# Strided rows for the blocks of two stacks, and the loads of one of them issued by ScalarE

## What is computed

```python
# layer 0
t  = layer_norm(x, g1, be1)
x  = x + softmax(q(t) @ k(t).T / 4 + mask) @ v(t) @ Wo.T + bo      # 16 heads
x  = x + ctx @ Wg.T + bg
x  = x + relu(layer_norm(x, g2, be2) @ W1.T + b1) @ W2.T + b2
# layer 1
t  = layer_norm(x, ln1_s, ln1_b)
x  = x + softmax(causal(q(t) @ k(t).T / 4)) @ v(t) @ wo
y  = layer_norm(x, ln2_s, ln2_b)
y  = x + softmax(q(y) @ k(ctx).T / 4) @ v(ctx) @ wo
z  = layer_norm(y, ln3_s, ln3_b)
out = y + relu(z @ mlp_w1 + mlp_b1) @ mlp_w2 + mlp_b2
```

## Time and profile before

| | us |
|---|---|
| median of 3 runs | 1675.22 |
| lowest, highest | 1666.01, 1680.92 |
| the profiled execution | 1690.34 |
| its span, first to last instruction | 1688.5 |
| PE, DVE, ACT, POOL busy in it | 1476.3, 1188.2, 1033.3, 837.5 |
| mean granted clock of PE | 0.953 |

### The profile page before, as it was taken

How to read it: one execution, slowest core, us unless ns; L and a number is a source line. 1 busy time by engine, 2 the same in 40 slices (tenths; PEclk the granted TensorE clock), 3 DMA queues, 4 the chain that set the end, 5 groups by cost and what they waited for, 6 DMA issues and landing times.

```text
span 1688.5 us, 43288 instructions
## 1 busy us (share of the span) xinstructions
PE 1476.3 (87%) x13568; PEld 1197.9 (71%) x13568; DVE 1188.2 (70%) x3871; ACT 1033.3 (61%) x2089; POOL 837.5 (50%) x1125
## 2 busy tenths in 40 slices
PE   2799999999999999778877778778999999999986
PEld 1578888888888888655655556555777777777756
DVE  2788878887878887666666666756776777677742
ACT  2677666677767675355545555556566656666652
POOL 4345544455545556643434343535555655565533
PEclk8799999999999999898889999998999999999989
DMA  5654644554555544456564755665644564446400
GB/s 135 151 126 111 130 104 100 118 107 100 126 115 119 115 101 131 104 128 121 103 121 95 129 104 120 136 134 113 117 104 98 117 119 94 105 113 113 86 26 13
DMA packets 163511, 185.76 MB, mean 110 GB/s; under 512 B 15952, under 2 KB 140240, under 8 KB 163408
## 3 DMA queue, kind: packets, MB, share of 16 engines
q1 hardware_dynamic: 163408, 184.57, 51.9%
HBM read 125.78 MB, written 58.72 MB: 109 GB/s over the span
## 4 chain that ended last, share of the span: by engine, by line
PE 55%; DMA 11%; ACT 9%; issue 8%; DVE 7%; SPq 5%; POOL 3%; ACTq 0%; DVEq 0%; POOLq 0%
PE d_ps L447 22%; DMA k_stack<-parts 9%; PE d_ps L708 8%; PE o_ps L582 7%; PE s_ps L504 6%; PE t_ps L518 5%; PE t_ps L552 3%; SPq L409 3%; DMA parts<-q_part 3%; SPq L414 2%; PE m_ps L454 2%; ACT prob_t L756 2%; POOL q_part L1128 1%; ACT q_stack L764 1%; POOL k_f L1128 1%
## 5 line engine op out<-in xcount | busy, mean ns | idle before, releaser
L756 ACT ACTIVATE prob_t<-t_ps 128x384 f32<-128x384 f32 (+1 forms) x512 | 275.4, 551 | 402.6 <-PE t_ps L556 204.0
L504 PE MATMUL s_ps<-k_stack,q_stack 96*128 96x256 bf16 (+1 forms) x1536 | 295.4, 275 | 125.8 <-DMA k_stack<-parts 58.6
L747 ACT ACTIVATE prob<-prob,neg_max 128x256 f32<-128x256 f32 x512 | 232.8, 507 | 124.5 <-DVE neg_max L908 121.6
L504 PEld LDWEIGHTS s_ps<-k_stack,q_stack 96*128 96x128 bf16 x1536 | 116.6, 100 | 228.4 <-issue 74.1
L908 DVE CUSTOM_DVE_ANT_0 prob<-s_ps,bias_sb 128x256 f32<-128x256 f32 x512 | 193.5, 417 | 55.3 <-PE s_ps L504 45.8
L552 PE MATMUL t_ps<-q_stack,k_stack 108*128 108x256 bf16 (+1 forms) x1024 | 209.3, 271 | 23.3 <-ACT prob_t L756 14.7
L1128 POOL TENSOR_TENSOR h_lo<-h_f,h_hi 128x512 fp32r<-128x512 f32 x128 | 164.9, 1288 | 123.1 <-DVE h_hi L1023 123.1
L908 DVE CUSTOM_DVE_ANT_0 prob<-s_ps,causal 128x128 f32<-128x128 f32 (+1 forms) x512 | 158.4, 351 | 93.8 <-PE s_ps L504 91.3
L893 DVE TENSOR_REDUCE top<-s_ps 128x2 f32<-128x512 f32 x256 | 172.9, 682 | 55.6 <-PE s_ps L504 51.8
L582 PE MATMUL o_ps<-prob_t,v_sb 128*17 128x256 f32 (+1 forms) x3072 | 204.2, 387 | 0.0
L447 PE MATMUL d_ps<-x2t_hi,w_hi 128*128 128x256 f32 x512 | 156.9, 306 | 14.8 <-ACT k_f L827 9.8
(11 more groups left out here) (127 smaller groups left out, 4062.1 us busy)
## 6 DMA issues: line engine op xcount, KB each, us to landing
q_stack<-parts SPq DMA_DIRECT2D x288, 128.0 KB, 4.2
k_stack<-parts SPq DMA_DIRECT2D x288, 128.0 KB, 6.9
parts<-q_part SPq DMA_DIRECT2D x96, 192.0 KB, 2.3
parts<-k_part SPq DMA_DIRECT2D x96, 192.0 KB, 2.3
ct_kept<-ct_hl SPq DMA_DIRECT2D x16, 512.0 KB, 8.5
x_in<-x_mid SPq DMA_DIRECT2D x32, 256.0 KB, 2.9
x_res<-x_mid SPq DMA_DIRECT2D x32, 256.0 KB, 2.9
ct_hl<-ct_kept SPq DMA_DIRECT2D x16, 512.0 KB, 8.1
```

Of the source, the lines that this page charges most:

```text
L504: last = mm(s_ps[:, h % 2, q * S:q * S + n], q_stack[0:ROWS, t.par, head_of(t, h), q * P:(q + 1) * P], k_stack[0:ROWS, t.par, head_of(t, h ...
L747: last = nc.scalar.activation(prob[:, h % 4, q, :], prob[:, h % 4, q, :], ACT.Exp, bias=neg_max[:, h % 4, q:q + 1], scale=-1.0)
L756: nc.scalar.activation(prob_t[:, h % 8, 0:n], t_ps[:, h % 2, 0:n], ACT.Exp, scale=-1.0)\
```

## The change

Two things. First, block j of either stack no longer takes 16 neighbouring rows (16j to 16j+15) but every sixth row from row j on (j, j+6, to j+90). The rows of both stacks are permuted alike, so each matmul sums the same 96 products. Second, the six loads of `k_stack`, with their wait for `k_written`, leave SP's slot 7 and are issued by ACT in slot 9, behind `h_f` and ahead of what else ACT does there. ACT also takes over a wait for the matmuls that last read the buffer. The loads of `q_stack` stay on SP.

```diff
                     for j, part in enumerate(Q_PARTS):
-                        sp.dma_start(q_stack[j * HD:(j + 1) * HD, t.par].rearrange("d (m h) s -> d m (h s)", m=KC),
+                        sp.dma_start(q_stack[j:ROWS:NBLK, t.par].rearrange("d (m h) s -> d m (h s)", m=KC),
                                      parts[t.par, 0, part].rearrange("m d h s -> d m (h s)")).then_inc(stacked.of(t), 16)
-                    sp.wait_ge(k_written.of(t), k_written.after(t))
-                    sp.sem_inc(passed, 1)
-                    for j, part in enumerate(K_PARTS):
-                        sp.dma_start(k_stack[j * HD:(j + 1) * HD, t.par].rearrange("d (m h) s -> d m (h s)", m=KC),
-                                     parts[t.par, 1, part].rearrange("m d h s -> d m (h s)")).then_inc(stacked.of(t), 16)
...
+                if h == 9 and has(st.nxt):
+                    t = st.nxt
+                    if st.prev:
+                        done = s_mm if has(st.prev, (0,)) else st_mm
+                        act.wait_ge(done.sem, done.after(st.prev))
+                        act.sem_inc(passed, 1)
+                    act.wait_ge(k_written.of(t), k_written.after(t))
+                    act.sem_inc(passed, 1)
+                    for j, part in enumerate(K_PARTS):
+                        nc.scalar.dma_start(k_stack[j:ROWS:NBLK, t.par].rearrange("d (m h) s -> d m (h s)", m=KC),
+                                     parts[t.par, 1, part].rearrange("m d h s -> d m (h s)")).then_inc(stacked.of(t), 16)
```

## The result

The changed kernel takes 1744.84 us (median of 4 runs, 1740.19 to 1745.35) against 1674.18 for the kernel before (4 runs): a ratio of 1.0418, 95% interval 1.0368 to 1.0468. It is 4.2% slower, and outside the range given. Its profiled execution has a span of 1743.5 us, 55 more than that of the kernel before, at a mean granted clock of 0.946. (The medians lie 71 us apart: the profiled execution of the kernel before was longer than its median.

The account below looks back on a forecast made before the run. It took PE to bound passes 0 and 2, and the late k_stack load pass 1. Terms -40.7 - 3.5 + 14 + 4 + 8 + 1 - 8 = -25.2 us took 1675.2 to 1650 us, range 1615 to 1704.

Parts of the forecast that it names:

- -40.7 (wait): Pass 1, slot 0: PE's 14 waits for the last k_stack load vanish whole, 40.7 us won.
- -3.5 (start): Kernel start: the first stack lands sooner with nothing to hide it, 3.5 us won of up to 4.2.
- +4 (layer norm): Pass 1, slot 0: the layer norm becomes the next wait, 0.3 us a step times 14, 4 us lost.
- -8 (clock): Pass 1: PE's granted clock recovers a fifth of the 39 us lost to its lower level, 8 us won.
- +14 (hold, pass 1): Pass 1: ACT's wait and issues make PE stall in slot 11, 14 us lost net.
- +8 (pass 0): Pass 0: ACT's issues delay prob_t and PE's transposes, 0.5 us a step times 16, 8 us lost.
- +1 (pass 2): Pass 2: ACT's issues end about when PE needs its pieces, 1 us lost over the pass.
- Net 0.5 to 2.1 a step; I take 1.0, times 14: Pass 1, slot 11: new 2.1 us stall, partly absorbing PE's DVE waits; 1.0 us a step net, 14 us lost.
- I take 2.7 on ACT too: Slot 9: six k issues take ACT 2.7 us, as on SP; bounds zero to 5.0 us.
- The third rival: All passes: dearer issues on ACT, ahead of PE's slot 11, cost 27 us per 0.1 us; 1704 at 0.62, chance 0.16.
- no faster landing: Rival: strided rows land no faster, the slot 0 wait stays and hides ACT's hold in pass 1; 1683 us, chance 0.13.
- The clock comes back: Rival, pass 1: without the slot 0 wait PE stays at 2.4 GHz, 31 us more won; 1619 us, chance 0.25.

Follow-up runs that it names:

- e1: Changed kernel with ACT's block removed: strided rows alone, all twelve loads issued by SP; 1641.46 us, 0.9726 of before.
- e9: e5's layout and wide q loads, but k in six loads of 16 neighbouring rows issued by ACT in slot 9; 1702.18 us, 1.0068 of before.
- e5: Against the changed kernel: parts laid out in DRAM for seven wide loads of neighbouring rows, all on SP; 1641.13 us, 0.9688 of before.
- e3: Changed kernel with ACT's six strided k loads spread, one at the end of each of slots 9 to 14; 1675.58 us, 0.9923 of before.
- e4: Against the changed kernel: all loads on SP, each block taking every second row of 32; 1641.68 us, 0.9728 of before.
- e2: Changed kernel with neighbouring rows for both stacks, ACT still issuing the k loads in slot 9; 1701.88 us, 1.0084 of before.
- e7: e1 plus ACT's two waits in slot 9, without any issue on ACT; 1636.72 us, 0.9674 of before.
- e10: e5 with its four wide k loads issued by ACT in slot 9; 1652.66 us, 0.9776 of before.
- e6: Changed kernel with ACT's waits and six issues moved to the end of slot 11; 1657.32 us, 0.9790 of before.
- e8: Changed kernel with three k loads back on SP and three left on ACT in slot 9; 1652.04 us, 0.9769 of before.

## Why the prediction was wrong

**Part one was right, in its sum partly by luck.** The prediction's terms for it are -40.7 (wait), -3.5 (start), +4 (layer norm) and -8 (clock), -48.2 in sum. The span of e1 is 1640.7 us against 1688.5, so -47.8. The load was in time and the wait in slot 0 is gone, by a smaller margin than thought: in the step shown the last load lands 9.6 us after the first issue, where 8.6 were forecast and 12.8 taken before, because the issues had become dearer. The start gave 1.8 instead of 3.5 (PE's wait for the first stack fell from 10.3 to 8.5 us, the first score from 41.9 to 40.6), and no wait for the layer norm appeared in PE's list. The wait was booked whole, but part of it came back in other places. Over the twelve steps 32.7 us of waiting for `k_stack` went, and this grew from 1.0 us:

```profile
PE t_ps L552 <- ACT prob_t L756: 11.7, 12, 1.0
```

so PE's idle time fell by 25.2 us only; its busy time fell by 9.3. For sixteen steps that is 34 and 12, with the start 48. The clock term was too small and the wait term too large, and the misses cancel.

**Part two was not.** Its terms were +14 (hold, pass 1), +8 (pass 0) and +1 (pass 2), +23 in sum. The difference of the changed kernel and e1 is +103. Two steps of the working failed, and the experiments size them apart.

*The first is "Net 0.5 to 2.1 a step; I take 1.0, times 14", with its pass 0 and pass 2 neighbours and the clock left out of it.* e9 has the very block that these terms assume. Against e5 it costs 16 x 0.93 = 15 us in pass 0 (8 taken), 16 x 2.44 = 39 in pass 1 (14 taken, 29 the upper end with 14 steps) and 16 x 0.37 = 6 in pass 2 (1 taken): 60 instead of 23. In pass 0 the step was within its bounds of 0 to 1.2, and the value near the middle was the wrong choice. In pass 1 it wasn't. The stall itself was found in the right place and size (2.1 us said, 2.1 to 2.4 measured in nine of twelve steps), and what it adds to PE's idle time against e5 is 1.6 us a step ((62.69 - 43.81) / 12), within the bounds. The rest of the 2.44, 0.9 us a step, is PE's busy time (266.69 us against 256.34 in e5's twelve steps), and for that the sum had no term: the clock was handled as a separate gain. "The longest idle time of a step moves from slot 0 to slot 11 rather than vanish" was seen, and only a recovery of 8 us was booked for it. With the block there is none: PE is busy for 266.69 us in twelve steps where it was for 264.04 before. The granted clock is 0.88, under the 0.93 that part one alone reaches and under the 0.90 of the earlier trace rows. That the clock falls behind the held slot 11 is counted above; that its fall costs the whole 0.9 us a step isn't shown, since e3 and e4 lose none at 0.91.

*The second is "I take 2.7 on ACT too".* The block measured 3.87 us in pass 1, since an issue takes 0.61 us and recurs every 0.65. e2 against the changed kernel sizes it: 1744.84 - 1701.88 = 43 us, on different chips, with a better landing on the side of the changed kernel. The third rival had the right mechanism for the whole, ACT ahead of PE's slot 11 in all passes, and its price rule roughly holds: 27 us for each 0.1 us, from 0.46 to 0.65, would be 51. (Its own figures don't follow that rule: from 0.46 the gain would be gone at 0.55, not at 0.52, and 0.62 would give 1693, not 1704; they are counted from the median duration of 0.42, not from the 0.46 that it names.) Its reason was wrong. It was not the arithmetic in ACT's queue: SP's issues of q, in the same kernel, take 0.59. What made them dear is part one itself, the step between the target rows; "Instructions, bytes and row lengths stay" had been taken to mean that the price stays. Why a strided target costs an issue 0.17 us more isn't settled by these runs, only that it does so on both engines, at steps of 2 and of 6, and not with 16 to 48 neighbouring rows.

**The rest.** Of the other rivals, "no faster landing" fell with e1. "The clock comes back" holds in no run: the granted clock in pass 1 is 0.93 in e1, 0.95 at most (e7), and 0.88 in the changed kernel. In the profile after, the stall in pass 1 of "about 2 us" was 3.3 to 4.8; in pass 0 "0.5 to 1.2" were 1.7. "It would be wrong if an issue on ACT takes clearly over 0.46" is what occurred. The cover of pass 2, called thin, was: 0.58 us a step against e1.

**How steep the cost is.** In the table, pass 1 takes 25.0, 25.5, 27.4 and 29.0 us a step for blocks of 0, 1.7 to 1.9, 2.7 and 3.9 us, at a granted clock of 0.93, 0.93, 0.91 (e2) or 0.88 (e9), and 0.88, and pass 0 takes 37.6, 37.7, 38.6 and 39.6. The cover of pass 0 is used up at about 1.9 us, and beyond it nearly every microsecond there, and more than one in pass 1, is PE's. The Trainium skill (DMA: Bandwidth & Descriptors, Issuing engines are not separate DMA queues) says that issuing from a second engine saves only issuing time. The runs agree in that no gain of the move shows: e1, without it, is the faster one by 103 us. What they add is that on an engine with a queue of arithmetic even this time isn't saved, but charged to whoever waits for that queue.

**Left open.** Where between the blocks of e10 and e9 the clock begins to fall in most steps was not tried, nor what its fall costs by itself, nor where 1.7 us of issues could stand in one block so that pass 1 has its 25.0. The 60 and 43 us come from kernels on different chips; the steps from their traces agree with them.

## What to carry to other kernels

When two edits come together, ask what each does to the unit price of the other: here the rows that make a load land sooner make its issue dearer, which costs nothing on SP and everything on ACT. A DMA issue on a compute engine is work of that engine: find what stands behind it in the queue and how much slack the consumer has there, and place it behind the last piece that someone waits for (e6 against the changed kernel: 88 us for two slots). And if a stall only moves on a PE whose clock is already lowered, don't book a recovery of the clock: here the stall in nearly every step left it at 0.88, where it had been 0.90.

## What was unexpected of the hardware

- An issue of a DMA from DRAM to 16 SBUF rows took a median of 0.59 us on SP and 0.61 on ACT (0.56 in e3, one at a time) with a step of 6 between the rows, 0.59 on SP with a step of 2, and 0.42 (SP) and 0.44 (ACT) with neighbouring rows; loads of 16 to 48 neighbouring rows cost the same 0.42.
- 16 rows spread over 32 landed almost as soon (2.8 us) as 16 spread over 96 (2.6 us); 16 neighbours had a median of 4.2 (q) and 6.9 (k).
- A stall of PE of 2.81 us in e8 left the granted clock at 1.00, behind the next one, of 2.86 us, it was 0.72 for 6 us; after one of 3.3 us in the changed kernel 0.53 for 6 us, and in e9 it was under 0.8 behind nine of twelve stalls, most of them of 2.1 to 2.4 us.
- A mean granted clock of 0.91 (e3, e4), 0.93 (e1) and 0.95 (e7) went with steps of pass 1 of 25.0, 25.0 and 24.9 us.
